# Image 0's fuse, sum, token and mixing stages placed in the gather loop of image 1

## The chip, the cores and the metric

One core of a Trainium2 chip runs the kernel. The metric is the device time of one execution in microseconds, the median over runs. The core has five engines that run their own instruction streams in order: PE (TensorE, matrix products; PEld are its weight loads), DVE (VectorE), ACT (ScalarE), POOL (GpSimd) and SP (SyncE, which only issues transfers). They meet at semaphores. Transfers run on 16 DMA engines; SP and ACT have a queue of their own each, and POOL issues the gathers.

## The reference, cut to what matters

Two images `x` of 128 channels and 64 x 64 pixels go through four deformable-convolution branches (7x7, 1x1, 1x1 and 3x3: 60 taps in all), then a fusing 1x1 convolution, a sum with `x`, and a spectral mixer over the 4096 tokens of each image.

```python
def deform_conv(x, off_w, off_b, mod_w, mod_b, reg_w, k, pad):
    offset = conv2d(x, off_w, off_b, pad)
    mask = 2.0 * sigmoid(conv2d(x, mod_w, mod_b, pad))
    sampled = bilinear_sample(x, py, px) * mask[:, None]     # py, px: pixel + tap + offset
    return einsum('bckhw,ock->bohw', sampled, reg_w.reshape(O, C, k * k))

x1..x4 = relu(group_norm(deform_conv(...)))                  # 256 channels each, over the image
x5 = relu(group_norm(conv2d(mean(x), pool_w)))
u = x + relu(group_norm(conv2d(concat(x1..x5), fuse_w)))     # fuse: 1280 -> 128 channels
# per token: layer norm, FFT convolution with 16 filters phi (U+, U-), then
out = sum_k U+ sigma_k^.25 M_phi_plus_k + U- sigma_k^.25 M_phi_minus_k + sum_i shift_i(u) M_u_i
```

`M_phi` and `M_u` are mixtures of four experts, weighted by a softmax over `log_weights + gumbel`; the weights do not depend on the image. A group norm needs a whole image, so an image's fusing can start only when all its branches are done; image 0 and image 1 do not depend on each other.

## The kernel before

**Order of the stages.** `program` runs blocks one after the other, each closed by a barrier of all engines: `stage_normalise` (image 0's layer norm and its table in DRAM), `stage_branches`, `stage_fuse`, `stage_sum`, `stage_tokens`, `stage_mixtures`, `stage_spectral`, `stage_output`.

**`stage_branches`** is one loop over `NT` = 960 steps, written out: 16 groups of 512 pixels (8 of image 0, steps 0 to 479, then 8 of image 1), 60 taps each. In step n = 60 g + k, POOL issues four indirect gathers (L509), each fetching for 128 pixels a row of 2 KB with the four corners of the sampling point; they go to one of `RING` = 6 buffers `G`, which is free again when blend n-6 is done (`blended`). ACT scales the first corner into PSUM (`corner0`, L541). DVE scales the other three (L666) and adds them up (L670, L674, L677: `blend`). PE transposes the result (`turn`, L779), ACT copies it out (`copy_out`, L549), and two steps later PE multiplies it by the tap's 128 x 256 weights (`contract`, L791). These weights stand in SBUF for all 60 taps: `R`, 60 KB in each partition. At the end of a branch ACT evacuates the sums (`evacuate`, L557), DVE takes their statistics (`measure`, L682) and SP stores them to `y_dram` (`store`, L432).

Other work is placed in the same loop by step numbers: the offset convolution of the next group (`convolve`, L761, in 52 of every 56 steps), its offsets and weights (`rows`, `weights`, spilled to DRAM by SP through the one buffer `om_next`: `spill`), and, in image 0's half, the layer norm and table of image 1 (`chunk_at`), whose PSUM bank `ps_s` is idle afterwards. `share_at`, `tile_at` and `chunk_at` give what is due at step n; each engine's loop calls the same functions with its own lateness. The block ends when all stores have landed; a second block clears six semaphores (L840 to L843).

**`stage_fuse`** handles both images, 16 groups g: SP loads `yin` (2.1 MB, four buffers, `load_y`, L959), ACT normalises and relus it (8 operations, L1062), PE sums 8 products (L1024), ACT copies out (L1042), DVE takes statistics (L1163). Between the groups stand image-independent pieces: the transforms of the filters `phi` (`kernel_transform`, 8 of them, rounded by ACT, split by DVE, stored to `kern_dram`), and the mixing of the expert weights (`mix`, L1148 to L1153, `split_mixed`) into `mh` and `ml`, and into `mus`. **`stage_sum`** adds `x` (L1227). **`stage_tokens`** runs 16 chunks of 4 x 128 tokens: transpose, layer norm, transpose back (`uT`), forward transform, split into high and low parts, three stores each (L1288), and for each image the edge bins (L1294). **`stage_mixtures`** makes 16 regions of `ps_m` from `uT` and `mus` (L1460), added by DVE (L1449) and stored by SP (L1441). `stage_spectral` and `stage_output` then read `spec_dram`, `kern_dram`, `mh`, `ml` and `t_dram`.

## Time and profile before

| what | us |
|---|---|
| median of 3 runs | 6341.98 (6341.73 to 6343.83) |
| the profiled execution | 6341.62 |
| its span, first to last instruction | 6339.8 |
| normalise and branches | 0 to 4938 |
| fuse, sum, tokens, mixtures | 4938 to 5281 |
| spectral | 5281 to 6288 |
| output | 6288 to the end |

Busy over the span: PE 5183.8 us (82%), DVE 4852.1 (77%), POOL 3943.7 (62%), ACT 2639.3 (42%). The mean granted TensorE clock was 0.937 of full speed. The gathers (line 509) are the costliest group of POOL: 3840 instructions, 953 ns in the mean.

How to read it: busy shares are means over stages with different limits, so the limit of each stage is read from stretches of the trace. POOL's busy time is the time in which it makes descriptors for the DMA engines, not the time of the transfer. The DMA share is the mean busy share of the 16 DMA engines. A PE matmul in fp32 stands as two records in the trace.

### The profile page before, as it was taken

How to read it: one execution, taken by the hardware profiler on the slowest of the kernel's cores; microseconds unless marked ns; L12 is line 12 of the kernel's file. 1: busy time of each engine (PE TensorE's matmuls, PEld its weight loads, DVE VectorE, ACT ScalarE, POOL GpSimd, SP SyncE). 2: the span in 40 equal slices, each digit the busy share in tenths (PEclk: the TensorE clock that was granted, in tenths of full speed). 3: DMA queues.
4: the chain of work that ended last, by engine and by line, in shares of the span. 5: the costliest groups of instructions: out<-in, count | busy, mean ns of one | idle time of the engine just before them, and what ended most of it. 6: DMA issues, size and time to landing. Idle time of an engine off the chain costs nothing. (4 is left out here: it accounts for less than half of the span.)

```text
span 6339.8 us, 66182 instructions
## 1 busy us (share of the span) xinstructions
PE 5183.8 (82%) x16608; PEld 2621.9 (41%) x16608; DVE 4852.1 (77%) x6696; ACT 2639.3 (42%) x6416; POOL 3943.7 (62%) x4379
## 2 busy tenths in 40 slices
PE   6987878888887888888787878875666759999998
PEld 5333333333333333333233333322222337777777
DVE  5897888878887888878788887878777364666664
ACT  1343434333333434333333333433333633666663
POOL 4777777777777777777777777777777002222221
PEclk8999999999999999999999999998888979999999
DMA  7777777777777777777777777777777864555555
GB/s 242 219 239 222 238 227 229 227 220 230 216 226 218 224 223 222 220 226 217 227 215 233 210 232 209 230 209 230 216 215 219 308 220 135 149 146 151 152 149 178
DMA packets 565020, 1349.89 MB, mean 213 GB/s; under 512 B 95111, under 2 KB 244490, under 8 KB 563338
## 3 DMA queue, kind: packets, MB, share of 16 engines
q0 software_dynamic: 328480, 1045.08, 56.4%
q1 hardware_dynamic: 216922, 282.50, 13.9%
q10 hardware_dynamic: 19344, 19.20, 0.9%
q8 instruction: 106, 1.74, 0.1%
q14 instruction: 168, 1.38, 0.1%
HBM read 1240.28 MB, written 106.13 MB: 212 GB/s over the span
## 5 line engine op out<-in xcount | busy, mean ns | idle before, releaser
L509 POOL DMA_INDIRECT G<-table,om x3840 | 3660.3, 953 | 1199.0 <-issue 1160.3
L666 DVE TENSOR_TENSOR G<-G,ps_w 128x1536 f32<-128x1536 f32 x960 | 1681.5, 1752 | 491.5 <-DMA G<-table,om 475.2
L791 PE MATMUL ps_y<-sT,R 128*128 128x512 f32 x3840 | 2015.7, 652 | 25.7 <-ACT yb L557 25.7
L541 ACT ACTIVATE ps_a<-G,om 128x128 f32<-128x128 f32 x3840 | 1192.6, 357 | 1871.6 <-DMA G<-table,om 1196.7
L779 PE MATMUL ps_t<-ident,acc 128*128 128x128 f32 x3840 | 661.9, 298 | 948.3 <-DVE acc L677 928.8
L779 PEld LDWEIGHTS ps_t<-ident,acc 128*128 128x128 f32 x3840 | 433.3, 147 | 1698.7 <-DVE acc L677 1587.0
L549 ACT ACTIVATE sT<-ps_t 128x512 f32<-128x512 f32 x960 | 572.1, 596 | 1073.3 <-PE ps_y L791 1070.8
L791 PEld LDWEIGHTS ps_y<-sT,R 128*128 128x128 f32 x3840 | 721.1, 208 | 592.6 <-issue 590.0
L1587 DVE TENSOR_TENSOR vl<-ps_v,vh 128x512 fp32r<-128x512 f32 x1024 | 657.4, 686 | 335.3 <-ACT vh L1536 335.1
L1521 POOL DMA_DIRECT2D ut<-spec_dram x512 | 262.5, 513 | 853.4 <-PE ps_v L1602 638.8
L670 DVE TENSOR_TENSOR ps_a<-G,ps_a 128x512 f32<-128x512 f32 x960 | 668.5, 696 | 131.6 <-ACT ps_a L541 32.9
L677 DVE TENSOR_TENSOR acc<-G,ps_a 128x512 f32<-128x512 f32 x960 | 659.8, 687 | 103.0 <-DVE ps_a L674 4.1
L1536 ACT ACTIVATE vh<-ps_v 128x512 fp32r<-128x512 f32 x1024 | 580.3, 596 | 356.7 <-PE ps_v L1602 331.3
L761 PE MATMUL ps_c<-xr,wom 128*128 128x512 f32 x1470 | 719.6, 610 | 0.0
L761 PE MATMUL ps_shared<-xr,wom 128*52 128x512 f32 x1470 | 718.5, 609 | 0.0
L674 DVE TENSOR_TENSOR ps_a<-G,ps_a 128x512 f32<-128x512 f32 x960 | 667.0, 695 | 31.8
L761 PEld LDWEIGHTS ps_c<-xr,wom 128*128 128x128 f32 x1470 | 292.2, 200 | 381.1 <-issue 381.1
L1625 PE MATMUL ps_yf<-vh,mh 128*128 128x512 f32 x1024 | 413.6, 404 | 0.0
L1625 PE MATMUL ps_yf<-vh,ml 128*128 128x512 f32 x1024 | 411.2, 402 | 0.0
L1625 PE MATMUL ps_yf<-vl,mh 128*128 128x512 f32 x1024 | 409.2, 400 | 0.0
L1602 PE MATMUL ps_v<-tt,ut 96*128 96x512 f32 x1024 | 367.9, 401 | 15.6 <-DMA ut<-spec_dram 13.8
L761 PEld LDWEIGHTS ps_shared<-xr,wom 128*52 128x52 f32 x1470 | 154.6, 126 | 503.2 <-issue 503.2
(187 smaller groups left out, 2386.4 us busy)
## 6 DMA issues: line engine op xcount, KB each, us to landing
tt<-kern_dram SPq DMA_DIRECT2D x512, 192.0 KB, 3.3
G<-table,om POOLq DMA_INDIRECT x3840, 3.7
y_dram<-yb SPq DMA_DIRECT2D x64, 512.0 KB, 4.8
yin<-y_dram SPq DMA_DIRECT2D x16, 2048.0 KB, 12.9
ut<-spec_dram POOLq DMA_DIRECT2D x256, 96.0 KB, 3.3
spec_dram<-spec_hi SPq DMA_DIRECT2D x64, 256.0 KB, 2.6
ut<-spec_dram POOLq DMA_DIRECT2D x256, 48.0 KB, 3.0
om_dram<-om_next SPq DMA_DIRECT2D x60, 150.0 KB, 3.5
```

Of the source, the lines that this page charges most:

```text
L509: pool.indirect_dma_start(G[k % RING][:, j, :], None, tables[g // GI], bass.IndirectOffsetOnAxis(ap=om[g % 2][:, j, 0, k:k + 1].bitcast(I3 ...
L541: last = nc.scalar.activation(ps_a[:, j, :], G[k % RING][:, j, 0:C], ACT.Copy, scale=om[g % 2][:, j, 1, k:k + 1])
L666: nc.vector.tensor_tensor(three, three, ps_w[:, :, h:h + 1].to_broadcast([128, 12, C]) .rearrange("p (j c) d -> p j c d", j=4), ALU.mult). ...
L670: nc.vector.tensor_tensor(ps_a[:, :, :], corner(1), ps_a[:, :, :], ALU.add).then_inc(added, 1)
L674: nc.vector.tensor_tensor(ps_a[:, :, :], corner(2), ps_a[:, :, :], ALU.add).then_inc(added, 1)
L677: nc.vector.tensor_tensor(acc[n % 3][:, :, :], corner(3), ps_a[:, :, :], ALU.add).then_inc(blended, 1)
L761: last = nc.tensor.matmul(ps_c2 if rest else ps_c[:, :], cols[:, 128:128 + REST] if rest else cols[:, 0:128], rows, start=(tap == 0), stop ...
L779: last = nc.tensor.transpose(ps_t[:, 128 * j:128 * j + 128], acc[n % 3][:, j, :], ident[:, :])
L791: last = nc.tensor.matmul(ps_y[:, half, :], R[:, k, 128 * half:128 * half + 128], sT[n % 2][:, :], start=(k == t0), stop=(k == ends[br] - 1))
L1536: nc.scalar.activation(vh[c][:, n, :, :], spread(ps_v[n % BANKS]), ACT.Copy).then_inc(v_high, 1)
L1587: nc.vector.tensor_tensor(vl[c][:, n, :, :], spread(ps_v[n % BANKS]), vh[c][:, n, :, :].bitcast(F32), ALU.subtract).then_inc(v_low, 1)
L1625: last = nc.tensor.matmul(ps_y[q][:, :], m[:, c, k, :], v[c][:, :, k, :], start=(c == 0 and k == 0 and n == 0), stop=(c == 1 and k == KF - ...
```

## The change

Image 0's part of the stages fuse, sum, tokens and mixtures, and the image-independent pieces (filter transforms, mixing of the expert weights), move into the loop of `stage_branches`, steps 486 to about 890, that is beside the gathers of image 1. The four stages behind the loop then handle image 1 alone (8 groups, 8 chunks, 8 regions).

- **Room.** The moved work needs SBUF, so the 60 KB of `R` become `arena`: in image 0's half it holds `R` as before, afterwards the buffers of the moved work. Image 1's contractions read their weights from a ring `RR` of three buffers with two taps each, loaded 240 times from DRAM through ACT's queue (`load_ring`), one load every second step.
- **One PSUM bank.** All moved work uses `ps_s` (here `side_ps`), one operation at a time. PE, ACT, DVE and SP get a function `side(n)`, called at the end of step n.
- **Schedule.** First step and spacing of each part: pooled mean and affine from 486; fusing 500 to 627, one product of 8 every second step; sum from 640, every second step; token chunks from 660, 12 steps each; mixtures from 760, 4 steps each; filter transforms from 793, 3 steps each; mixing of `M_phi` from 822, 8 steps for each of 8 slices (`KM` = 2 filters at a time, before 4). `mw` is now in PSUM, and `combine` copies one half of it out before it adds and subtracts.
- **Through DRAM.** `mus`, `mh` and `ml` are stored to `mus_dram` and `m_dram` and loaded again in `stage_fuse` through POOL's queue, together with `fuse_w`.
- **Class `Fusion`** holds the small operations of the fusing's statistics, for both uses; `gp` and `gf` (norm parameters) are loaded with the constants at the start.
- **Clearing.** The block behind the loop clears all semaphores of `stage_branches`: 125, before 6.

The core of the diff (`side` on the other engines, and the moved operations themselves, are of the same form as those shown):

```diff
-def stage_branches(nc, x, xn, tables, wom, R, ps_shared, base, P, rowt, regw, ident, eps6, om_dram, y_dram, ystats, xpart):
+def every(n, first, step, count):
+    i, late = divmod(n - first, step)
+    return i if late == 0 and 0 <= i < count else None
...
+def stage_branches(nc, d, xn, tables, wom, arena, R, ps_shared, base, P, rowt, ident, eps6, eps5, blk16, blk8,
+                   om_dram, y_dram, ystats, xpart, gp, gf, fa, fb, hot, spec_dram, kern_dram, t_dram, mus_dram, m_dram):
...
+        split = Carve(arena[:, 0:FU_AT])
...
+        mw = side_ps.rearrange("c (k s e) -> c k s e", k=KM, s=2)
...
+        FIRST = GI * TAPS
+        FS, SS, TT, TP, MM, MP, WK, KP, WM, WP = 500, 640, 660, 12, 760, 4, 793, 3, 822, 8
...
+            def load_y(m):
+                g, i = divmod(m, 2 * NBR)
+                if m == 0:
+                    for h in range(3):
+                        sp.wait_ge(stored[h], 16 + 16 * YB.count(h) * GI)
+                if m >= 4:
+                    sp.wait_ge(fused, m - 3)
+                sp.dma_start(yin[m % 4], y_dram[g, i // 2, i % 2]).then_inc(y_loaded[m % 4], 16)
...
+            def store_spec(c, half):
+                p, q = chunks[c]
+                sp.wait_ge(lo_ready, 2 * c + half + 1)
+                for h, t, _ in PARTS:
+                    sp.dma_start(bins(spec_dram, 0, half, h, (S + 1) * p + 4 * q, 4), t[:, half, :].bitcast(F32))\
+                        .then_inc(spec_stored[half], 16)
...
+            def load_ring(q):
+                if q >= RSLOTS:
+                    act.wait_ge(summed, FIRST + RTAPS * (q - RSLOTS + 1))
+                k = RTAPS * q % TAPS
+                act.dma_start(RR[q % RSLOTS][:], regw[:, k:k + RTAPS, :]).then_inc(rr_loaded[q % RSLOTS], 16)
+
...
+            def round_spec(c, half):
+                act.wait_ge(transformed, 2 * c + half + 1)
+                if c:
+                    act.wait_ge(spec_stored[half], 48 * c)
+                nc.scalar.activation(hi[:, half, :], side_ps, ACT.Copy).then_inc(hi_ready, 1)
...
+                q = every(n, FIRST - 1, RTAPS, GI * TAPS // RTAPS)
+                if q is not None:
+                    load_ring(q)
...
+                for half in range(2):
+                    c = every(n, TT + 8 + 3 * half, TP, NCH)
+                    if c is not None:
+                        round_spec(c, half)
...
+            def split_spec(c, half):
+                dve.wait_ge(hi_ready, 2 * c + half + 1)
+                nc.vector.tensor_tensor(lo[:, half, :], side_ps, hi[:, half, :].bitcast(F32), ALU.subtract)\
+                    .then_inc(lo_ready, 1)
...
+            def mix(c, i):
+                if i == 0:
+                    dve.wait_ge(m_loaded[c % 2], 16 * (c // 2) + 16)
+                    ws.then(nc.vector.tensor_scalar(mw, mr[c % 2][:, :, :, 0, :], wi[:, 0:1], None, ALU.mult))
+                else:
+                    ws.then(nc.vector.scalar_tensor_tensor(mw, mr[c % 2][:, :, :, i, :], wi[:, i:i + 1], mw,
+                                                           ALU.mult, ALU.add))
...
+                if n == FIRST + 6:
+                    dve.wait_ge(measured, NBR * GI + 2)
+                    dve.wait_ge(summed, FIRST)
+                    f.dve_means(dve)
...
+                    segment_weights()
+                i = every(n, FS + 4, 1, SEG)
+                if i is not None:
+                    segment_mixture(i)
...
+                for i in range(SEG):
+                    c = every(n, WM + i, WP, NM)
+                    if c is not None:
+                        mix(c, i)
...
+                if g < GI:
+                    taps = R[:, k, :]
+                else:
+                    q = (n - FIRST) // RTAPS
+                    if k % RTAPS == 0:
+                        pe.wait_ge(rr_loaded[q % RSLOTS], 16 * (q // RSLOTS) + 16)
+                    taps = RR[q % RSLOTS][:, k % RTAPS, :]
                 for half in range(2):
-                    last = nc.tensor.matmul(ps_y[:, half, :], R[:, k, 128 * half:128 * half + 128],
...
+            def fuse(m):
+                g, i = divmod(m, 2 * NBR)
+                pe.wait_ge(z_ready, m + 1)
+                if m == 0:
+                    pe.wait_ge(f.b5_ready, 1)
+                if i == 0 and g:
+                    pe.wait_ge(fu_ready, g)
+                nc.tensor.matmul(side_ps, fw[:, i, :], yin[m % 4], start=(i == 0), stop=(i == 2 * NBR - 1)).then_inc(fused, 1)
...
+                m = every(n, FS, 2, 2 * NBR * GI)
+                if m is not None:
+                    fuse(m)
+                if n == FS + 4 * NBR * GI + 5:
...
             def _(sp):
-                for s in [xn_turned, xn_copied, xn_summed, xn_stored, table_written, ln_step]:
+                for s in sems:
                     sp.sem_clear(s)
...
+        @block.gpsimd
+        def _(pool):
+            pool.dma_start(fw[:], fuse_w).then_inc(fw_loaded, 16)
+            pool.dma_start(flat(mus[:]), mus_dram).then_inc(mus_loaded, 16)
+            pool.wait_ge(z_ready, GI)
+            for i, t in ((0, mh), (1, ml)):
+                pool.dma_start(flat(t[:]).bitcast(F32), m_dram[i].rearrange("c s k e -> c (s k e)")).then_inc(m_loaded, 16)
...
+            for g in range(GI):
                 sp.wait_ge(fused, g + 1)
-                sp.dma_start(yin[g % YR][:], y_dram[g].rearrange("b h p n -> p (b h) n")).then_inc(y_loaded[g % YR], 16)
...
+                sp.dma_start(yin[g % YR][:], y_dram[GI * b + g].rearrange("b h p n -> p (b h) n")).then_inc(y_loaded[g % YR], 16)
...
```

## Rows read from the trace of the kernel before

**Rows 1.** The page, busy tenths of GpSimd in 40 equal slices.
```profile
POOL 4777777777777777777777777777777002222221
```
**Rows 2.** Line 509, the gathers: duration, idle before them, landing.
```profile
L509 POOL DMA_INDIRECT G<-table,om x3840: 947/953/1046, 64.9 to 4919.2; - x192
...
  issue: 1160.3, 3807
...
  DVE acc L677: 13.2, 29
...
DMA to landing us min/median/max: 3.2/3.7/10.1
```
**Rows 3.** Stretches: us, busy (count) PE, PEld, DVE, ACT, POOL, PEclk, DMA share, GB/s.
```profile
2606.00:3256.00 650.00, 536.23 (x1522) 221.79 (x1520) 543.30 (x697) 249.41 (x681) 492.41 (x518) 0.96 0.75 222
4226.00:4550.00 324.00, 198.48 (x542) 86.57 (x540) 265.44 (x332) 122.81 (x334) 245.56 (x258) 0.86 0.74 219
4955.00:4960.00 5.00, 3.13 (x4) 1.51 (x5) 0.00 (x0) 5.00 (x8) 0.00 (x0) 0.50 1.05 387
4938.00:5281.50 343.50, 233.01 (x868) 137.84 (x868) 152.24 (x410) 159.69 (x262) 0.11 (x1) 0.87 0.68 249
```
**Rows 4.** Timeline, PE in one step: start, us, instruction, [idle before, releaser].
```profile
3915.58 0.66 PE L779 MATMUL ps_t<-ident,acc 128*128 128x128 f32 x4 [0.25 <-DVE acc L677]
3916.07 1.88 PE L791 MATMUL ps_y<-sT,R 128*128 128x512 f32 x4
3917.89 1.94 PE L761 MATMUL ps_shared<-xr,wom 128*52 128x512 f32 x4
```
**Rows 5.** Timeline, the first instructions of the stages behind the gathers.
```profile
4938.68 0.35 SPq L953 DMA_DIRECT2D pw<-in_pool_w  x1
...
4940.49 12.47 SPq L959 DMA_DIRECT2D yin<-y_dram  x4
...
4951.07 11.38 ACT L1062 ACTIVATE yin<-yin,ybb,ya 128x512 f32<-128x512 f32 x16 [4.11 <-DMA yin<-y_dram]
...
5101.32 17.42 SPq L1209 DMA_DIRECT2D t_xg<-in_x  x16
...
5123.06 0.33 SPq L1282 DMA_DIRECT2D fwd<-in_dft  x1
...
5219.52 56.43 PE L1460 MATMUL ps_m<-uT,mus 128*128 128x64 f32 x384 [12.30 <-PEq L1235]
...
5281.53 18.93 SPq L1510 DMA_DIRECT2D tt<-kern_dram  x16
```
**Rows 6.** Timeline, ACT's copies of fused groups: the first and the last two.
```profile
4965.65 0.69 ACT L1042 ACTIVATE fu<-ps_f,bias 128x512 f32<-128x512 f32 x1 [3.20 <-PE ps_f L1024]
...
5087.27 0.69 ACT L1042 ACTIVATE fu<-ps_f,bias 128x512 f32<-128x512 f32 x1 [0.55 <-PE ps_f L1024]
...
5094.14 0.69 ACT L1042 ACTIVATE fu<-ps_f,bias 128x512 f32<-128x512 f32 x1 [0.71 <-PE ps_f L1024]
```
**Rows 7.** Sum, edge-bin stores of each image, mixtures: lines and timeline.
```profile
L1227 DVE TENSOR_TENSOR accum<-t_rb,t_xg x16: 1043/1100/1132, 5104.4 to 5121.5; 128x512 f32<-128x512 f32 x16
...
5173.72 1.52 SPq L1294 DMA_DIRECT2D spec_dram<-edge_hi  x2
...
5213.77 1.27 SPq L1294 DMA_DIRECT2D spec_dram<-edge_hi  x2
...
L1449 DVE TENSOR_TENSOR accum<-accum,ps_m x16: 686/687/690, 5226.3 to 5276.0; 128x512 f32<-128x512 f32 x16
```
**Rows 8.** SyncE's barriers around the first stage's 24 clears; issue of constant loads.
```profile
L244 SPq EVENT_SEMAPHORE x1: 17/17/17, 57.2 to 57.2; - x1
...
L245 SPq DRAIN x1: 7/7/7, 59.2 to 59.2; - x1
...
L1762 SPq DMA_DIRECT2D blk<-in_blk x2: 421/426/432, 1.3 to 1.8; - x2
```
**Rows 9.** The groups by line, the largest of the weight mixing: busy, mean ns.
```profile
L1150 DVE SCALAR_TENSOR_TENSOR mw<-mr,wi,mw 128x1024 f32<-128x1024 f32 x12 | 15.4, 1285 | 0.4
```
**Rows 10.** Around 60 us: GB/s in 1.5 us slices of 60:120; gathers; landing of xw.
```profile
GB/s 358 382 382 382 406 382 426 413 342 412 405 382 110 34 42 223 203 310 349 286 53 26 25 34 197 183 208 232 199 284 273 535 307 512 299 408 403 292 112 0
...
68.81 0.95 POOL L509 DMA_INDIRECT G<-table,om  x1 [0.30 <-issue]
...
DMA to landing us min/median/max: 3.9/6.0/12.7
```

More of the change, by code:

```diff
@@ L3 @@
 from contextlib import ExitStack
+import math
 B, C, H, W = 2, 128, 64, 64
@@ L359, in stage_branches @@
+        QS = S // 4
+        chunks = [(p, q) for p in range(2) for q in range(QS)]
+        NCH = len(chunks)
+        PARTS = ((0, hi, ehi), (1, hi, ehi), (2, lo, elo))
+        NC = CH // (2 * S)
+        kernels = [(q, c) for q in range(4) for c in range(2)]
+        NK, NM = len(kernels), KF // KM
         NT = NG * TAPS
@@ L602, in _ @@
                     copy_x(c)
+                side(n)
         @block.vector
@@ new lines, in turn_u, with transform @@
+            def turn_u(c):
+                pe.wait_ge(u_ready, c + 1)
+                for j in range(4):
+                    last = nc.tensor.transpose(ps_s[:, j, :], un[:, j, :], ident[:, :])
+                last.then_inc(u_turned, 1)
+            def transform(c, half):
+                if half == 0:
+                    pe.wait_ge(uT_ready, c + 1)
+                    pe.wait_ge(dft_loaded, 32)
+                else:
+                    pe.wait_ge(lo_ready, 2 * c + 1)
+                nc.tensor.matmul(side_ps, fwd[:, half, :], flat(un), start=True, stop=True).then_inc(transformed, 1)
@@ new lines, in transform_edge, with mix_region @@
+            def transform_edge():
+                pe.wait_ge(lo_ready, 2 * NCH)
+                for half in range(2):
+                    last = nc.tensor.matmul(ps_s[:, half, :], fwd_edge[:, half, :], un[:, 3, :], start=True, stop=True)
+                last.then_inc(edge_done, 1)
+            def mix_region(r, late):
+                p, q = chunks[r]
+                if r == 0:
+                    pe.wait_ge(edge_zeroed, 1)
+                    pe.wait_ge(mus_ready, SEG)
+                    pe.wait_ge(elo_ready, 1)
+                elif not late:
+                    pe.wait_ge(m_added, r)
+                last = mix_tokens(nc, ps_s, mus, uT, p, q, SEGMENTS[SEG - 1:] if late else SEGMENTS[:SEG - 1])
+                if late:
+                    last.then_inc(mixed, 1)
@@ L1421, with mix_tokens, stage_mixtures @@
 SEGMENTS = ((0, 16, 0), (16, 32, 1), (32, 64, 2), (64, 128, 3))
-def stage_mixtures(nc, accum, uT, mus, t_dram):
+def mix_tokens(nc, out, mus, uT, p, q, segments):
+    for lo, hi, seg in segments:
+        for lag in range(3):
+            src, shift = (p - lag) % 2, (p - lag) // 2
+            s0 = 1 + 4 * q + shift
+            last = nc.tensor.matmul(out[:, :, lo:hi], mus[:, lag, seg, :], uT[:, src, s0:s0 + 4, lo:hi],
+                                    start=(lo == 0 and lag == 0), stop=(lag == 2), skip_group_check=True)
+    return last
+def stage_mixtures(nc, b, accum, uT, mus, mus_loaded, t_dram):
     ctx = ExitStack()
```

1033 lines of the change are left out of this document (674 added, 359 removed).

## Prediction

> **What bounds the kernel now.** I read three views in this order. The page's slices first: through slice 31, to 4913 us, GpSimd holds a flat 7 (after a slower first slice) [rows 1], while the digits of the other engines move. Then the gather line alone: the 3840 gathers take 947 to 1046 ns each, 1160 us of GpSimd's idle time there is "issue" in 3807 pieces (0.3 us each), and only 13.2 us is spent waiting for a finished blend [rows 2]. So a gather costs 0.953 + 0.30 = 1.255 us, and a step (four gathers: one tap of 512 pixels) 5.02 us. Then the stretches: 518 gathers in 650 us, 258 in 324, although TensorE is busy 82% of the one and 61% of the other [rows 3]. GpSimd's own issuing paces the first 4935 us. VectorE is busy 543 of 650 us [rows 3], 4.20 of 5.02 a step: 0.8 are spare. TensorE at full clock works 4.25 us of a step with convolution [rows 4]. ScalarE is busy 249 of 650, 1.9 a step [rows 3].
>
> The ring of six gather buffers gives slack in time. When blend n starts, some 3.7 us after its last gather was issued [rows 2], GpSimd is about to issue step n+2, which needs blend n-4; so some 3.4 steps, 17 us, may be lost by VectorE before a gather is held up.
>
> Behind it the stages run one after the other, with nothing beside them [rows 5]: fuse from 4938.7 to 5101.3 (162.6 us), sum to 5123.1 (21.8), tokens to 5219.5 (96.4), mixtures to 5281.5 (62.0), together 342.8; then the spectral stage and the output, untouched.
>
> **The change, part by part.** The sum is made against the profiled execution, 6341.6 us (span 6339.8), 0.4 below the median of the runs shown.
>
> *Fuse, in the tail.* It keeps 8 of 16 groups and loses the kernel transforms and the mixing of weights. The first load of y is issued 0.4 us into the stage, not 1.8, and was in use 10.6 us after its issue [rows 5]. fuse_w and mus now come at the same time by GpSimd's queue: 1.4 MB, at the 387 GB/s which the DMA engines reach in this stage [rows 3] up to 3.7 us more, of which I take 1. First relu at 12.0. From it to the first group out 14.6 us [rows 5, 6]. Then 7 groups at 6.87, the spacing of the last ones, between which no kernel transform stood [rows 6]: 48.1. Copy and statistics 1.4, the small chain 3.8. 12.0 + 14.6 + 48.1 + 1.4 + 3.8 = 79.9: **82.7 saved**. A group is 2.1 MB, 5.4 us at 387 GB/s, so loading stays under TensorE's 6.87.
>
> *Sum.* 16 additions from 5104.4 to 5122.6 are 1.14 apart [rows 7]; 8 fewer: **9.1 saved**. *Tokens.* The stores of the edge bins close an image, the first at 5173.72, the second at 5213.77 [rows 7]: **40.1 saved**. *Mixtures.* 16 additions from 5226.3 to 5276.0 are 3.31 apart [rows 7]: **26.4 saved**. The 4.2 MB of mh and ml are loaded once the last relu is done, 11 us at 387 GB/s, and wanted over 100 us later: nothing, at most 5 us where they crowd the loads of x. Tail: 158.3.
>
> *Clearing semaphores.* The block behind the gathers clears 6 semaphores now and, counted in the diff, 125 then. SyncE does it between two barriers, with nothing beside it. The 24 clears of the first stage took from 57.2 to 59.2, 83 ns each [rows 8]. 119 x 0.083 = **9.9 us added**. Two more constants are loaded at the start, 0.43 us of issue each [rows 8], before the first stage may begin: **0.9 added**.
>
> *What goes under the gathers (steps 486 to 890 of 960).* The whole tail has VectorE busy for 152 us, TensorE 233 and ScalarE 160 [rows 3]. Image 1 keeps on VectorE 8 statistics x 0.69, 8 additions x 1.10, 8 token chunks x 4.1, 8 x 0.69 and 9 of small work, 62; so 90 move, and small work done twice and copies out of PSUM make it about 104. Spare: 0.8 x 404 = 320. TensorE: fusing 8 x 6.87, mixtures 8 x 3.31, chunks and kernels 33: 114, of about the same spare. ScalarE: 84 move, some 20 of table loads and 240 ring loads at 0.43 of issue are new, 207 in all, of 1250. GpSimd gets nothing. The dense stretches: VectorE in the weight mixing (steps 822 to 886) has 265.4 of 324 us now, 4.12 a step [rows 3], and gets 33 us (12 operations at 1.28 [rows 9], and as much again in others) over 64 steps, 0.52: 4.64 of 5.02. TensorE in the mixtures (760 to 792) has 4.25, and 3.31 over four steps is 0.83: 5.08, over the pace by 0.06 for some 24 steps, 1.5 us, which the ring takes.
>
> *Added waits.* All side work shares one PSUM bank, passed from engine to engine, and most steps of it stand one to three steps behind what they need. Queued behind a wait on VectorE is the next blend, behind one on ScalarE the first corner of the next step, behind one on TensorE the transpose on which ScalarE waits. The longest pieces are the segment weights on VectorE (20 dependent operations, some 4 us) and the roots on ScalarE with two table loads, some 3 us: each once, against 17 us of slack. SyncE gets some 200 more issues; its loads run 4 or more steps ahead, but a spill of offsets must land within a step and a half, and a side wait ahead of it could cost VectorE 1 to 3 us, 28 times, regained at 0.8 a step.
>
> *The ring of weights.* 131 KB a step is 26 GB/s: at 387 for the whole, 0.07 of the DMA engines, on 0.75 [rows 3]. The loads of y add 0.07 more in steps 500 to 628 (0.89), the mixing of weights 39 GB/s, 0.10, in steps 822 to 886 (0.92). Each load (two taps, 262 KB) is issued three steps, 15 us, before its use; one of the same size, beside the gathers, took 6.0 us at the median and 12.7 at most [rows 10]. Bounds for all that image 1's gathers may lose: not below zero, for the gathers are as many and GpSimd sets their pace; above, 200 loaded steps at 5% over, 50 us. I take **3**, near the low end, because with the DMA engines at 340 to 420 GB/s and gathers landing up to 10.1 us after issue, they were still issued 1.26 apart [rows 2, 10].
>
> The Trainium skill, page "DMA: Bandwidth & Descriptors", section "SWDGE vs HWDGE vs iDMA", says that a DMA engine takes its software-fed and its hardware-fed queues in turn. By that, side loads delay gathers well below full load; by the rows a landing of 10.1 instead of 3.7 is 6.4 us once, inside the slack, and the sum stays.
>
> Sum: 6341.6 - 158.3 + 9.9 + 0.9 + 3 = **6197.1 us**.
>
> **The rivals.**
> (a) *The gathers become DMA-bound.* For: 0.75 is a mean, and the load reaches 0.9. Against: the traffic beside gathers in [rows 10]. Price: 50 us instead of 3, 6244.
> (b) *GpSimd is held up by the moved VectorE work.* If every moved operation stopped it for its length, 104 us: 6298. Against: VectorE is busy 84% and GpSimd 76% of the same stretch [rows 3], which could not be then, and the longest gather issue is 1046 ns [rows 2]. The Trainium skill, page "SBUF — State Buffer", section "SBUF: two separate sides", has a narrower rule: VectorE in its fast modes locks GpSimd out of writing descriptors; most of the moved operations read PSUM.
> (c) *Slower than before: the hand-offs of the one bank stall the step.* The place is ScalarE: VectorE waits for a rounding of the same step, which stands behind a copy, an evacuation and a ring load. Beyond the spare 0.8 us a step, each further us costs 404 us over the 404 steps. From 0.36 beyond it (145 / 404) the change is slower than before; at 0.6 beyond it, 6194 + 242 = 6436. Against: ScalarE is free for 3 us of each step [rows 3], and such waits stand in some 35 steps only.
> (d) *It doesn't do what it says:* side work overruns the last gather. Its last step is 890 of 960, 350 us early; only (c) could bring it there.
>
> **How the numbers follow.** Forecast, 6183 to 6215: 0.66. Between that and (a), up to 6250: 0.15. Below 6183 (a quicker start of fuse, cheaper clears): 0.07. Above 6250 and still faster, (b) among it: 0.06. (c): 0.05; about no change: 0.01. The range 6183 to 6250 holds 0.81. 0.2% is 12.7 us, about what a measurement of this kernel can tell from no change. Faster 0.94, same 0.01, slower 0.05.
>
> **What would show it.** In the profile after: gathers 1.255 us apart through image 1, with less than 20 us of waits for VectorE; the last contraction near 4936; 10 us between the barriers of the clearing block; fuse 80, sum 13, tokens 56, mixtures 36 us. If the gathers of steps 500 to 628 stand further apart while the DMA share is 0.95 or more, it is (a); if they wait for blends, and VectorE for ScalarE or TensorE, it is (c). A fuse of over 90 us would say that loading bounds it.

## The result

| | median, us | ratio to the kernel before |
|---|---|---|
| before | 6341.85 (6339.43 to 6343.83) | |
| changed | 6202.34 (6201.74 to 6202.94) | 0.978, 95% interval 0.9763 to 0.9797 |

The change saves 139.5 us; 144.5 were forecast. The profiled executions have spans of 6339.8 and 6200.1 us.

The gathers of the changed kernel, to be read against [rows 2], from the groups of instructions:

```profile
L747 POOL DMA_INDIRECT G<-table,om x3840 | 3663.2, 954 | 1205.7 <-issue 1154.8 <-DVE acc L1023 26.2 <-DVEq L995 24.8
```

and from the view of their line (shortest, median and longest duration in ns, first and last start in us):

```profile
L747 POOL DMA_INDIRECT G<-table,om x3840: 947/953/1872, 64.6 to 4928.6; - x192
```

GpSimd still sets the pace: 1154.8 us of issue, as before. But waits for a finished blend are 26.2 us instead of 13.2, the longest gather takes 1872 ns instead of 1046, and the last gather begins at 4928.6 instead of 4919.2. GpSimd's idle time before gathers grew from 1199.0 to 1205.7 us and the gathers themselves from 3660.3 to 3663.2, together 9.6 us.

Image 1's stretches in the changed kernel (us; busy time and instructions of PE, PEld, DVE, ACT, POOL; granted clock, DMA share, GB/s), against [rows 3]:

```profile
2606.00:3256.00 650.00, 587.27 (x1655) 252.64 (x1655) 552.23 (x734) 297.62 (x761) 492.23 (x517) 0.96 0.86 275
3881.00:4041.00 160.00, 140.52 (x469) 65.47 (x467) 132.48 (x190) 61.15 (x164) 121.29 (x128) 0.95 0.84 265
4226.00:4550.00 324.00, 201.43 (x544) 87.25 (x544) 297.89 (x401) 127.04 (x347) 242.89 (x255) 0.85 0.86 279
```

517 gathers in 650 us, where 518 stood before, although the DMA share rose to 0.86. In the weight mixing (third row) 255 stand for 258: three gathers, nearly 4 us, were lost.

Behind the gathers, the changed kernel's timeline (start, us, engine, line): the last store of image 1's branches, the first load of fuse, the first relu, and the first loads of sum, tokens and spectral:

```profile
4946.07 0.36 SPq L561 DMA_DIRECT2D y_dram<-yb  x1
...
4957.18 0.35 SPq L1632 DMA_DIRECT2D pw<-in_pool_w  x1
...
4970.02 11.38 ACT L1672 ACTIVATE yin<-yin,f_small 128x512 f32<-128x512 f32 x16 [7.30 <-DMA yin<-y_dram]
...
5038.82 7.72 SPq L1716 DMA_DIRECT2D t_xg<-in_x  x8
...
5050.99 0.33 SPq L1787 DMA_DIRECT2D fwd<-in_dft  x1
...
5141.93 188.47 SPq L2017 DMA_DIRECT2D tt<-kern_dram  x104
```

and, from the views of two lines, the clears and the copies out of the fusing:

```profile
L1455 SPq EVENT_SEMAPHORE_RANGE_CLEAR  x125: 25/30/35, 4949.3 to 4956.9; - x125
...
L1665 ACT ACTIVATE fu<-ps_f,f_small x8: 687/687/687, 4984.5 to 5032.6; 128x512 f32<-128x512 f32 x8
```

With the starts of [rows 5] this gives the whole difference of the two spans (us):

| piece | forecast | measured | from |
|---|---|---|---|
| start of the gathers | +0.9 | -0.3 | 64.6 for 64.9 |
| first to last gather | +3 | +9.7 | 4864.0 for 4854.3 |
| last gather to last store | 0 | +1.9 | 17.5 for 15.6 |
| last store to fuse (clears) | +9.9 | +7.2 | 11.1 for 3.9 |
| fuse | -82.7 | -81.0 | 81.6 for 162.6 |
| sum | -9.1 | -9.6 | 12.2 for 21.7 |
| tokens and mixtures | -66.5 | -67.5 | 90.9 for 158.5 |
| spectral, output | 0 | -0.1 | 1058.2 for 1058.3 |
| sum | -144.5 | -139.7 | |

### The profile page after: what moved, and what is told of

Read it like the earlier page. It is cut to its first block and busy times, and to the rows that moved or that the text cites. A ratio compares the mean times of both kernels' runs of the same rounds, so it can differ in the third digit from the quotient of the medians.

```text
span 6200.1 us, 67010 instructions
## 1 busy us (share of the span) xinstructions
PE 5157.6 (83%) x16620; PEld 2629.0 (42%) x16620; DVE 4855.8 (78%) x6768; ACT 2642.2 (43%) x6429; POOL 3948.8 (64%) x4383
## 3 DMA queue, kind: packets, MB, share of 16 engines
q1 hardware_dynamic: 224538, 287.87, 14.5%
## 5 line engine op out<-in xcount | busy, mean ns | idle before, releaser
L747 POOL DMA_INDIRECT G<-table,om x3840 | 3663.2, 954 | 1205.7 <-issue 1154.8
L1307 PE MATMUL ps_y<-sT,RR 128*128 128x512 f32 x1920 | 1030.0, 665 | 17.7 <-issue 9.2
L1307 PE MATMUL ps_y<-sT,arena 128*128 128x512 f32 x1920 | 977.5, 635 | 5.5 <-ACT yb L795 5.5
L1307 PEld LDWEIGHTS ps_y<-sT,RR 128*128 128x128 f32 x1920 | 370.9, 214 | 308.8 <-issue 307.0
L1307 PEld LDWEIGHTS ps_y<-sT,arena 128*128 128x128 f32 x1920 | 350.8, 203 | 279.4 <-issue 279.4
```

The source lines that it names most:

```text
L747: pool.indirect_dma_start(G[k % RING][:, j, :], None, tables[g // GI], bass.IndirectOffsetOnAxis(ap=om[g % 2][:, j, 0, k:k + 1].bitcast(I3 ...
L1307: last = nc.tensor.matmul(ps_y[:, half, :], taps[:, 128 * half:128 * half + 128], sT[n % 2][:, :], start=(k == t0), stop=(k == ends[br] - 1))
```

## The experiments

The theory: GpSimd's issuing sets the pace of image 1, and what the gathers lose, they lose at single places. The rivals are (a), (b) and (c) of the prediction. The runs stand on three chips: e1 to e4 on one, e5 to e8 on another, e9 to e12 on the third. The kernel before ran on each, so results are compared by their ratio to it, or, where the effect is under 10 us, by rows of their profiles. Run e9 is the changed kernel once more: 6205.68 us, ratio 0.9782 (0.9769 to 0.9796); that is the anchor for the ratios. A ratio's interval is 9 to 13 us wide to each side, so no ratio alone shows a smaller difference.

### Where the gathers were lost: the end of a burst

Two waits stand out in the changed kernel, near 3765 and 4330. VectorE's last operation of each blend around the first, with the token chunk's statistics and normalisation (in order of time; the offset rows and weights of steps 716 to 723 lie between them):

```profile
3724.86 0.69 DVE L1023 TENSOR_TENSOR acc<-G,ps_a 128x512 f32<-128x512 f32 x1
...
3732.81 0.69 DVE L1023 TENSOR_TENSOR acc<-G,ps_a 128x512 f32<-128x512 f32 x1
...
3752.17 0.69 DVE L1023 TENSOR_TENSOR acc<-G,ps_a 128x512 f32<-128x512 f32 x1
...
3755.97 0.89 DVE L1100 BATCH_NORM_STATS2 arena<-ps_side 128x6 f32<-128x128 f32 x4
3756.90 0.38 DVE L1103 BATCH_NORM_AGGREGATE arena<-arena 128x2 f32<-128x6 f32 x4
...
3762.87 1.37 DVE L1110 TENSOR_SCALAR arena<-ps_side,arena 128x128 f32<-128x128 f32 x4
...
3767.54 0.69 DVE L1023 TENSOR_TENSOR acc<-G,ps_a 128x512 f32<-128x512 f32 x1
```

and GpSimd beside it:

```profile
3757.85 0.95 POOL L747 DMA_INDIRECT G<-table,om  x1 [0.31 <-issue]
3761.51 0.95 POOL L747 DMA_INDIRECT G<-table,om  x1 [2.71 <-DVE acc L1023]
...
3768.50 0.95 POOL L747 DMA_INDIRECT G<-table,om  x1 [2.27 <-DVE acc L1023]
```

From 3724.86 to 3767.54 six steps take 42.7 us, 7.1 each, against GpSimd's 5.02: 12.5 us of the ring's 17 go in six steps, on top of what the steps before had used. In the kernel before, the same six steps (last operations at 3720.55 and 3762.05) took 41.5 us: the burst was there, and the side work in and just before it came on top. The mean over 650 us shows nothing of it.

Of each wait for a blend, 0.30 us would pass at issue in any case. From the list of GpSimd's waits between 2600 and 4930 us (total, number), what lies beyond that is 1.1 us in the kernel before (5.0 us, 13 waits) and 8.5 in the changed one (16.6 us, 27 waits).

**e2** moves all side work behind the sum by some steps:

```diff
-        FS, SS, TT, TP, MM, MP, WK, KP, WM, WP = 500, 640, 660, 12, 760, 4, 793, 3, 822, 8
+        FS, SS, TT, TP, MM, MP, WK, KP, WM, WP = 500, 640, 666, 12, 766, 4, 799, 3, 838, 8
```

> The changed kernel with token chunks, mixtures and kernel transforms 6 steps later and the mixing of the weights 16 steps later (838 instead of 822), nothing else. Theory: most of the 9.4 us that the gathers lost is lost where VectorE's bursts of offset rows and weights (steps 716 to 723 and 828 to 835, some 6.7 us of work a step instead of 5.02 to the gathers) use up the slack of the ring, and a token chunk or the mixing of weights falls on the end of them: the gathers waited for a blend 5.4 us near 3760 and 4.2 us near 4330. With both collisions moved away, waits for VectorE fall from 26 to under 18 us, the last gather starts 6 to 9 us earlier, near 4921, and the kernel takes 6194 to 6197. Rival: the gathers lose to the DMA engines' load (0.86 to 0.89 of them busy), which the shift leaves as it is: 6201 to 6204, and the waits move with the work.

Measured: 6203.05 us, ratio 0.977 (0.9754 to 0.9786). The median lies in the range of the expectation's rival, and the last gather begins at 4929.1, not near 4921. All waits for VectorE together are 27.4 us, where under 18 were expected. The wait near 4330 is gone: 398 gathers between 4065 and 4565 where the changed kernel has 395. The one near 3765 stayed (2.99 us), since the statistics of another chunk now fell on steps 716 and 717, and a smaller one came at 4048 (1.11 us). The expectation of 6 to 9 us was wrong: I had reckoned with the end of the burst and not with its beginning, where the same slack is spent. That the waits move with the work, at the same DMA share (0.86 from 4065 to 4565), speaks for the theory; what the shift was worth in time is small (the table further down).

### The gathers that take longer

Some gathers themselves take up to 1.87 us. One of them, and VectorE beside it (timeline of the changed kernel):

```profile
3402.13 1.87 POOL L747 DMA_INDIRECT G<-table,om  x1 [0.30 <-issue]
...
3402.02 1.14 DVE L1092 TENSOR_TENSOR arena<-arena 128x512 f32<-128x512 f32 x1
```

The addition ends at 3403.16 and the gather at 3404.00, 0.84 us later: but for 0.1 us at its start, the gather's 0.95 lie behind the addition. The same holds within 0.03 us for the other four that begin beside one of the sum's eight additions (1.11, 1.12, 1.31 and 1.66 us); all of these additions read only SBUF and write SBUF. The statistics of 3768.14, which have one operand in SBUF, leave the gather of 3768.50 at 0.95.

The kernel before shows the same in small. 16 of its gathers, besides the first, take over 1.0 us, and each begins beside a VectorE operation of 128x120 or 128x60 with both operands in SBUF. 15 of them begin 0.07 or 0.08 us after the start of one and the same operation (L629); the 4 gathers that begin within its first 0.02 us keep their 0.95. One of the pairs:

```profile
3172.13 0.28 DVE L629 TENSOR_TENSOR fr<-P,fl 128x120 f32<-128x120 f32 x1
3172.21 1.03 POOL L509 DMA_INDIRECT G<-table,om  x1 [0.30 <-issue]
```

This gather, too, ends 0.83 us after the operation; since the operation takes only 0.28, it costs 0.08.

**e5** lets the relu write PSUM, so that the addition reads one operand there:

```diff
-                nc.scalar.activation(v, v, ACT.Relu, bias=f.fb, scale=f.fa).then_inc(relu_ready, 1)
+                if k:
+                    act.wait_ge(t_added, k)
+                nc.scalar.activation(side_ps, fu[:, k * CH:k * CH + CH], ACT.Relu, bias=f.fb, scale=f.fa)\
+                    .then_inc(relu_ready, 1)
...
+                nc.vector.tensor_tensor(accum[:, :, :, k * NC:k * NC + NC], by_block(side_ps),
```

> The changed kernel with the relu of image 0's eight sum steps (640 to 656) written to the side bank of PSUM instead of in place, so that each of VectorE's eight additions reads one operand from PSUM and one from SBUF; their number and their place stay. In the changed kernel's trace five gathers that begin while such an addition runs take 1.11 to 1.87 us instead of 0.95, and each ends later by the rest of the addition less 0.1 us; all other gathers take 0.95. Theory: an operation of VectorE whose operands and result are all in SBUF holds back the gather that begins beside it, one that touches PSUM doesn't. So the additions take about 1.1 us as before, the stretched gathers between 3320 and 3410 are gone, and the gathers end 2 to 3 us earlier; the whole 6199 to 6201 (the whole alone can hardly show it). Rival: the DMA engines' load at that place (loads of x and of y) delays them; then the long gathers stay.

Measured: 6205.55 us (6200.59 to 6210.51), ratio 0.9787 (0.9767 to 0.9806), which can't show 3 us. The profile does:

```profile
L1094 DVE TENSOR_TENSOR arena<-ps_side,arena x4: 1039/1040/1047, 3343.6 to 3408.9; 128x512 f32<-128x512 f32 x4
L747 POOL DMA_INDIRECT G<-table,om x3840: 950/957/1284, 64.2 to 4937.6; - x192
```

The additions take 1.04 us in the same places, and no gather between 3320 and 3410 is over 1.1 us. 73 gathers stand there instead of 70, at a DMA share of 0.83 instead of 0.82. In e5 only two gathers begin well inside an addition (over 0.2 us before its end), so the other runs count: in the ten traces with the additions of the changed kernel, 49 gathers begin so, and 48 of them take 1.06 to 2.25 us; 47 end 0.81 to 0.86 us after the addition, one 1.16, behind which stands the added operation of e8. (The one exception, in e7, begins 0.03 us after the addition and takes 0.96.) In the three with an operand in PSUM (e5, e6, e10), 11 begin so and all take 0.95 or 0.96. So the operands made the gathers long. The longest gather left in e5, 1284 ns, begins beside one of the segment weights' operations, 0.61 us long and with two SBUF operands.

**e7** and **e8** price the same in a pair: one more addition of 128x256 in each of 404 steps, with one operand in PSUM (e7) or both in SBUF (e8).

```diff
+                if FIRST + 6 <= n < FIRST + 410:
+                    dve.wait_ge(weights_spread, (n + 1) // HALF_TAPS + 1)
+                    for e in range(1):
+                        ex.then(nc.vector.tensor_tensor(flat(xnp[:])[:, 0:256], <wom>, <ps_w or wom>, ALU.add))
```

> The changed kernel with one more VectorE addition of 128x256 in each of steps 486 to 889, one operand from PSUM, one from SBUF, result into SBUF; it computes nothing that is used. Pair with the next run. At 0.35 to 0.4 us each it brings 404 x 0.4 = 160 us of VectorE work where, by the rows, 0.8 a step were spare and the moved work takes 0.26 of it on average. Theory: the gathers keep their 0.95 us; the collisions with the bursts of offset rows lose more, up to 1.3 us of recovery a step less: the time grows by 5 to 40 us, all of it in waits for blends.

> The same with both operands of the added operation in SBUF; nothing else differs from the run before. Theory of the held gathers: the operation takes 0.5 to 0.55 us, and the gather that begins beside it is stretched by up to its length: a mean of 0.2 us over 0.53 / 1.255 of 404 operations would be 35 us, twice that if blends and gathers run in step; so many gathers of 1.0 to 1.5 us in image 1 and a time 20 to 80 us above the run before. Rival: gathers stay at 0.95 us and the two runs differ only by the operation's own length, 404 x 0.15 us at most where no slack is left.

Measured: 6243.74 us, ratio 0.9847 (0.9827 to 0.9867), and 6243.23 us, ratio 0.9846 (0.9827 to 0.9866). The view of the added operation's line in e7, then in e8, then one of e8's held gathers with it (timeline):

```profile
L1253 DVE TENSOR_TENSOR xnp<-wom,ps_w x404: 385/415/433, 2558.0 to 4644.1; 128x256 f32<-128x256 f32 x135
```

```profile
L1253 DVE TENSOR_TENSOR xnp<-wom x404: 392/419/482, 2550.1 to 4638.3; 128x256 f32<-128x256 f32 x135
```

```profile
4283.37 0.42 DVE L1253 TENSOR_TENSOR xnp<-wom 128x256 f32<-128x256 f32 x1
...
4283.44 1.18 POOL L748 DMA_INDIRECT G<-table,om  x1 [0.31 <-issue]
```

Gathers over 1.0 us: 27 in e7 (27 in the changed kernel as well), 114 in e8, and together they are 4.5 and 17.3 us over 0.953. The operation takes the same 0.42 us in both forms, where 0.5 to 0.55 were expected of e8. So the hold is real, and small: most gathers don't begin beside the addition, and each is held only for what is left of it. It cost e8 nothing in the end, where I had expected 20 to 80 us: waits for blends are 59.0 us in e8 and 67.1 in e7, so that a held gather seems mostly to have taken the place of a wait. From image 1's first gather to its last, e8 takes 2464.9 us and e7 2463.8. e7's own cost, 0.0065 of 6341, 41 us, is at the upper end of the 5 to 40 expected, and its interval is 13 us wide to each side.

### How much VectorE has to spare

**e12** does e7's addition twice a step.

```diff
-                    for e in range(1):
+                    for e in range(2):
```

> The changed kernel with two of the added VectorE additions (0.415 us each, one operand from PSUM) in each of steps 486 to 889: 335 us of VectorE work, 0.83 a step. One of them cost about 40 us, in waits for blends near the bursts of offset rows. Theory: spare are 0.8 a step less 0.26 for the moved work, 0.54; one added operation leaves 0.12, two are over by 0.29 in every step: the gathers are paced by VectorE from end to end of the 404 steps, and the time grows by 0.29 x 404 = 117 us and the 40 of the bursts, 120 to 200 us over the changed kernel, with thousands of short waits gone into hundreds of waits for VectorE. Rival: spare is more than the rows say, because VectorE's waits between the operations of a blend can take the work: 60 to 100 us.

Measured: 6406.01 us, ratio 1.0097 (1.0078 to 1.0115): slower than before, 200 us over e9 on the same chip. The end of the expected range, so the spare is less than reckoned. The stretch of e12:

```profile
2606.00:3256.00 650.00, 546.26 (x1492) 225.84 (x1493) 600.71 (x924) 275.53 (x689) 451.81 (x474) 0.95 0.79 253
```

474 gathers are 118.5 steps of 5.49 us, and VectorE is busy 5.07 of each. It is the bound here: its list of waits names none for a gather in this stretch, where the changed kernel has 35.7 us of them. It is still idle for 0.42 us a step, in gaps within and between the blends that other work doesn't fill. (GpSimd waits only 31 times in these 650 us, 63.1 us in all; between 2690 and 2820 104 gathers come 1.25 us apart, while VectorE, at some 4.9 us a step, makes up a little of what the bursts cost.) e7 gives the same, and again VectorE waits for no gather: 593.98 us busy over 128 steps of 5.08, a gap of 0.44. The changed kernel's 552.23 over 129.25 steps is 4.27; 5.02 - 0.42 - 4.27 leaves **0.33** a step. Over 404 steps that is 133 us; added work of 335 and 168 us less the measured 200 and 41 gives 135 and 127.

### The DMA engines, and the queue of the ring

**e11** copies each load of the ring a second time, to a spare place in DRAM.

```diff
                 act.dma_start(RR[q % RSLOTS][:], regw[:, k:k + RTAPS, :]).then_inc(rr_loaded[q % RSLOTS], 16)
+                for e in range(1):
+                    act.dma_start(spare[q, e], regw[:, k:k + RTAPS, :].rearrange("c t o -> c (t o)"))\
+                        .then_inc(spare_written, 16)
```

> The changed kernel with each load of the ring of weights doubled: ScalarE's queue issues beside it a copy of the same 256 KB to a spare place in DRAM, 240 times, 26 GB/s more, 0.07 of the DMA engines by the prediction's price. The DMA share, 0.84 to 0.87 in image 1, should go to 0.92 to 0.96. Theory: GpSimd's issuing still sets the pace, so the gathers stay 1.255 us apart, waits for VectorE grow by at most 10 us, and the time by at most 10. Rival (a), that the gathers are near the DMA bound: landings pass the ring's slack, VectorE waits for gathers and GpSimd for blends, and the time grows by 50 us or more.

Measured: 6207.63 us, ratio 0.9784 (0.9766 to 0.9802), 2 us over e9. Two stretches of e11:

```profile
2606.00:3256.00 650.00, 588.85 (x1651) 250.12 (x1650) 549.44 (x731) 303.13 (x757) 491.45 (x515) 0.95 0.90 301
4080.00:4226.00 146.00, 138.61 (x423) 58.69 (x422) 123.97 (x136) 61.31 (x166) 110.59 (x116) 1.00 0.93 318
```

With the DMA engines busy at 0.90 to 0.93 (0.92 to 0.96 were expected), 515 gathers stand in the stretch that had 517, and they land after 3.9 us at the median and 10.2 at most (3.8 and 10.0 in the changed kernel). Rival (a) is out up to this share, and the change itself stays at 0.86.

**e4** issues the ring from SyncE's queue instead of ScalarE's (`sp.dma_start` in SyncE's `side`, nothing else).

> The changed kernel with the loads of the ring of contraction weights issued by SyncE's queue instead of ScalarE's. ScalarE is rid of 240 issues (0.34 us each), SyncE gets them, each with its wait for a contraction, ahead of the spills of offsets, the loads of y and the stores of the side work. Theory: ScalarE has 3 us free of 5 in a step, so what it gains is worth nothing; a load waits for the contraction two steps back, done when SyncE comes to it in its own order, so SyncE loses little: within 2 us of 6202.3. Rival: SyncE's in-order waits come late for the spills and the loads of y, VectorE waits for spills, and the bursts lose more: 6207 or more, with VectorE's waits for spilled offsets in the trace.

Measured: 6211.06 us (6206.38 to 6213.83), ratio 0.9783 (0.9767 to 0.9799). By the ratios there is no difference, and VectorE's waits hold no spill. The median, 6211.06, is where the rival of the expectation had it (6207 or more), but on a chip on which the kernel before is 4.7 us slower, too. Its profiled execution, with a span of 6212.0 us, has its last gather at 4940.5. Image 1's gathers take 6.1 us more there than in e1 on the same chip (2431.9 for 2425.8), and some 3 of these are gathers held beside the sum's additions, which happened to fall together more often (six of eight, up to 1.94 us); whether any of the rest is the queue's is left open.

### The clears, and a better kernel

**e1** clears the 125 semaphores, whose numbers are consecutive, in one instruction.

```diff
-                for s in sems:
-                    sp.sem_clear(s)
+                sp.sem_clear(range(first, last + 1))
```

> The changed kernel with its 125 semaphores (they have consecutive numbers) cleared by one instruction. In the trace of the changed kernel the 125 clears run from 4949.3 to 4956.9, 61 ns apart. Theory: they lie on the path between two barriers, so the kernel ends 124 x 0.061 = 7.6 us earlier, near 6194.7, and the fuse stage begins near 4949.6 instead of 4957.18. By the step of the prediction (83 ns a clear) it would be 10.3 us. Rival: SyncE would wait anyway for the landing of the last store (issued at 4946.07), or one clear of a range takes as long as its parts: then the time stays within 1 us of 6202.3.

Measured: 6201.61 us (6197.4 to 6204.6), ratio 0.9772 (0.9756 to 0.9788). The last of the stores begins at 4946.45 and fuse at 4950.23:

```profile
4950.23 0.35 SPq L1633 DMA_DIRECT2D pw<-in_pool_w  x1
```

3.8 us for 11.1, and 3.9 in the kernel before with its six clears: the 125 cost 7.3 us, and one instruction for all costs no more than the six did.

**e3** joins e1 and e2.

> The two edits together: one clear, and the shifted steps. Theory: they stand at different places on the path and add up, 7.6 + 6 to 9 us, so 6186 to 6189. If the shift brings nothing: 6194 to 6195.

Measured: 6198.09 us, ratio 0.9765 (0.9748 to 0.9781), 11 us under the anchor's ratio where 14 to 17 were expected. The clears' part is there (4948.32 to 4952.09, 3.8 us, from the last store to fuse), so what is missing is e2's.

**e6** is e1 and e5 with a hole in the token chunks instead of a shift, so that none stands in the burst:

```diff
+        GAP = 16
+        def chunk_of(n, late):
+            c = every(n, TT + late, TP, NCH // 2)
+            if c is not None:
+                return c
+            c = every(n, TT + TP * (NCH // 2) + GAP + late, TP, NCH // 2)
+            return None if c is None else c + NCH // 2
```

> The changed kernel with one clear, with the sum's additions reading PSUM, with the token chunks 4 to 7 started 16 steps later, so that none of their VectorE work lies in steps 712 to 725 (branch statistics at 714, offset rows and weights 716 to 723), mixtures and kernel transforms 16 later, and the weights mixed from step 838. Shifting all chunks by 6 steps left the wait near 3765 (2.99 us against 2.71), since a chunk's statistics then fell on steps 716 and 717; the wait near 4330 went. Theory: waits for VectorE in image 1 fall to those of the kernel before (2.2 us near 3760) plus the 0.6 to 1.5 near 2655, no gather of image 1 takes over 1.4 us, the gathers end 5 to 8 us earlier than in the changed kernel, and with the clear's 7.3 the time is 13 us under the changed kernel's: ratio to the kernel before 0.9760 to 0.9765 after 0.9780. Rival: the ring's slack is lost elsewhere as soon as work is put elsewhere; then ratio 0.977.

Measured: 6190.92 us, ratio 0.9763 (0.9746 to 0.9779). In image 1 the waits for VectorE are 12.3 us in all, and the longest 1.1 (changed kernel: 16.6 and 3.3; before: 5.0 and 0.9), and no gather takes over 1.30 us. This is as expected.

**e10** adds one clear for the first stage and moves the load of `mus` behind two groups of y; **e9** is its anchor.

```diff
+            pool.wait_ge(z_ready, 2)
             pool.dma_start(flat(mus[:]), mus_dram).then_inc(mus_loaded, 16)
```

> The changed kernel itself, as an anchor on the chip of the next three runs, since the gathers of one and the same line took between 3661 and 3674 us in all on different chips. All theories: ratio to the kernel before 0.978, within 0.001.

> The run with all three edits (one clear, the sum's additions from PSUM, the schedule with a gap of 16 steps), and two more: the 24 semaphores of the first stage cleared by one instruction as well (1.8 us by the 2 us that they take), and the loads of image 1's segment mixture (0.77 MB) issued once two groups of y are through the relu instead of first in the fuse stage, where the first relu waited for y until 12.8 us into the stage. Theory: 7.3 + 1.8 from clears, 3 to 6 in the gathers, 1 to 2 from the first relu (0.77 MB at 387 GB/s is 2.0 us): 13 to 17 us under the changed kernel on the same chip, ratio to before 0.9755 to 0.976. Rival: the load of y is held by its own queue and not by the bytes beside it: the first relu stays at 12.8 us; then 12 to 15.

Measured on one chip: e10 6186.04 us (6183.91 to 6186.65), ratio 0.975 (0.9737 to 0.9763), e9 6205.68 (6203.16 to 6207.69). The view of the gathers' line and the timeline (first load of fuse, first relu) of e9:

```profile
L747 POOL DMA_INDIRECT G<-table,om x3840: 947/953/1674, 63.7 to 4930.5; - x192
```

```profile
4956.97 0.35 SPq L1632 DMA_DIRECT2D pw<-in_pool_w  x1
...
4970.74 11.38 ACT L1672 ACTIVATE yin<-yin,f_small 128x512 f32<-128x512 f32 x16 [8.22 <-DMA yin<-y_dram]
```

and the same of e10:

```profile
L754 POOL DMA_INDIRECT G<-table,om x3840: 949/953/1301, 62.2 to 4920.8; - x192
```

```profile
4940.38 0.35 SPq L1643 DMA_DIRECT2D pw<-in_pool_w  x1
...
4951.53 11.38 ACT L1683 ACTIVATE yin<-yin,f_small 128x512 f32<-128x512 f32 x16 [5.51 <-DMA yin<-y_dram]
```

The gathers begin 1.5 us earlier and take 8.2 less, fuse starts another 6.9 earlier behind them (7.3 of the clears), and the first relu comes 11.2 instead of 13.8 us into the stage: 19.4 with the rest of fuse, of which 2.8 lie there. The median is 19.6 us lower, and 159.0 under the chip's median of the original kernel (6345.07). That is more than the 13 to 17 us expected: the gathers gave more than the 3 to 6, and the first relu more than the 1 to 2.

The table has the time from the start of image 1's first gather to that of its last, and the waits for blends beyond the 0.30 us each, for pairs on one chip. The kernel before has 2414.8 and 1.1.

| run | image 1's gathers, us | waits beyond 0.30, us |
|---|---|---|
| e1, then e2 | 2425.8, 2424.1 | 10.8, 4.9 |
| e5, then e6 | 2429.5, 2421.2 | 9.6, 2.1 |
| e9, then e10 | 2426.8, 2418.9 | 9.2, 4.4 |

The hole in the token chunks (e6) took 7.5 us of waits away and the stretch became 8.3 us shorter. In e2, 5.9 us fewer waits brought 1.7, while the gathers of the whole run took 6.8 us more (3668.4 for 3661.6), for which no cause is shown. Of e10's 7.9, 4.8 are waits and 2 are held gathers; the last us is not explained, and the sum of all gathers' lengths differs by 2.3 us between two executions of one kernel (3663.2 in the changed kernel, 3665.5 in e9).

## Why the prediction was right

**The sum.** The total is off by 4.8 us, and in part by luck: the pieces that came out longer than forecast make 10.3 us (gathers 6.7, last store 1.9, fuse 1.7), those that came out shorter 5.5 (clears 2.7, constants 1.2, tokens and mixtures 1.0, sum 0.5, the rest 0.1).

**Pace and tail.** The forecast case held: GpSimd's issuing bounds image 1, the side work goes under it, and the tail halves. Fuse (79.9 forecast, 81.6), sum (12.7, 12.2), tokens and mixtures (92.0, 90.9) came out within 2 us each. In fuse, first relu to first group (14.5 for 14.6) and the seven spacings (48.1 for 48.1) were right. The term that was off is the first relu, 12.8 us into the stage instead of 12.0, and the end, 6.2 us for 5.2 after the last copy out. I took 1 us for the loads that come beside y; in e9 it was 13.8 us, and e10, with `mus` later, had 11.2, so 1.7 to 2.6 would have been the price of `mus` alone.

**Clears: mechanism right, size off.** 83 ns from 24 clears gave 9.9 us; 125 in a row stand 61 ns apart (7.6 / 124), so a longer row of them is cheaper for each than the 24 of [rows 8]; why is not shown. e1 prices them at 7.3.

**The constants.** +0.9 was forecast, -0.3 measured, below what two executions can tell.

**Gathers: +3 forecast, +9.7 measured.** The bounds, 0 to 50, held it. The step that failed is "VectorE 4.20 of 5.02 a step: 0.8 are spare". Two things are wrong in it. Of the idle 0.8, 0.42 can't be used (e12, e7); what the 404 steps took without loss was 0.33 each. And a mean over 650 us hides the bursts of offset rows, in which VectorE takes 7.1 us a step: in the kernel before, GpSimd already waited 0.6 and 0.85 us at the end of the one near 3760, so there the 17 us of slack were all but gone, and any added operation counts in full. The prediction asked only whether its own long pieces (4 us, 3 us) fit into 17. e6 shows the collisions going when the work moves; e2 removed one of the two. The 3 was set by the landings of the gathers, and these have no part in the loss: they are 3.8 us at the median and 10.0 at most, before 3.7 and 10.1. The stretched gathers are a second, smaller part: 2.9 us in the line's busy time.

**The wait for spills.** 1 to 3 us, 28 times, were set for it as regained; none appears among VectorE's waits. PE in the mixtures was busy 140.5 of 160 us, 4.41 a step, where 5.08 was forecast: in the kernel before it was 121.4 in the same 160 us, so 3.81 a step and not the 4.25 of a full step with convolution was the base, and 0.60 came on top instead of 0.83. Neither touched the sum. VectorE in the weight mixing, 4.64 forecast, was 4.67 (297.89 us over 63.75 steps).

**Last gather to last store**, +1.9: the profiled execution's TensorE was granted a mean of 0.72 of its clock from 4936 to 4942, so part of it at the lower level of 1.2 GHz, where the kernel before had 1.00 from 4926 to 4932, at the same point of its work. The engine had been idle for 2.08 us before. Its last twelve products take 7.01 us there and 5.32 in e9, which was granted 1.00; in e9 the piece is 15.4 us, so it isn't the change's.

**Rival (a)** is out by e11: at 0.90 to 0.93 at most some 2 us are lost (image 1's gathers take 2428.6 us for 2426.8 in e9). The shares forecast for image 1, 0.89 and 0.92, were 0.86 and 0.86.

**Rival (b)** has its mechanism, but not its size. Moved VectorE work does hold GpSimd where both operands are in SBUF and a gather begins beside it, as in five of eight additions of the sum. Two other groups that were moved have two SBUF operands: the mixing of `mus` (three operations of 0.61 us, one gather of 1.31) and the low parts `ml` (16 of 0.48 us, three gathers of up to 1.21). All else reads PSUM or only one operand from SBUF or is short, so 3 to 4 us were at stake and not 104. The argument against it, that the longest gather of before was 1046 ns, was a misreading: the gathers of 1.01 to 1.04 us were held ones, and they were short because the old loop had no such operation longer than about 0.3 us. The prediction took one half of what the Trainium skill says, page "SBUF — State Buffer", section "SBUF: two separate sides": beside the fast modes it names operations with two SBUF inputs, against a GpSimd instruction that reads SBUF. By that half the eight additions would have been listed, at up to 1.1 us each; e5 and e8 agree with it.

**Rival (c)** is real further out. Its threshold, 0.36 us beyond the spare, was right in kind: e12, with 0.83 more a step and 0.33 to spare, is 0.5 beyond and 1% slower than before (1.0078 to 1.0115). This tests the price and not the mechanism: e12 loads VectorE and leaves the hand-offs alone. In the changed kernel, between 2430 and 4930 us, VectorE's waits for ScalarE's first corner grew from 5.4 to 23.5 us, and its waits for the side work's roundings are 10.1 us. They did not stall the step: VectorE still waited 177 us for gathers there.

## What to carry to other kernels

Where an engine's idle time is to be filled, read it at the worst burst beside the resource it feeds, not from a stretch's mean; and take off the gaps inside its own chain, which the engine keeps even when it is the bound. If the kernel before already waits at the end of a burst, however shortly, nothing more belongs there. Long operations that VectorE does beside GpSimd's gathers should read at least one operand from PSUM; it is worth little (some 2 us here), and nothing measurable where the gathers wait for blends anyway (e8).

## What the runs showed of the hardware beyond the forecast

- A gather (0.95 us) that begins while VectorE works on two SBUF operands, but for the last 0.1 us, ends 0.81 to 0.86 us after that operation (rows of 3402 and 3172 above; 47 of 49 in ten runs, and e8); with one operand in PSUM it keeps its 0.95 (11 of 11 in e5, e6 and e10), and so it does beside statistics with a single SBUF operand (3768.50).
- VectorE, as the bound, with some eight operations a step (924 in 118.5 steps), is busy for 92% of the time (e12: 600.7 of 650 us).
- Semaphores cleared one by one in a row cost 61 ns each; a range of 125 in one instruction costs no more than the six of before did (3.8 us from the last store to fuse, 3.9 before).
- GpSimd's pace holds up to a DMA share of 0.93: 1.26 us a gather (e11: 116 in 146 us at 0.93, 515 in 650 us at 0.90).
